# A semaphore wait in front of each of 432 embedding gathers

## What is computed

```python
e = jnp.stack([tbl_f[ids[:, f]] for f in range(40)], axis=1)      # (2048, 40, 32)
vi = e[:, _I_IDX, :]                                              # the 780 pairs i < j
vj = e[:, _J_IDX, :]
z = jnp.einsum('bke,kef,bkf->bk', vi, W, vj)                      # (2048, 780)
h = jnp.concatenate([z, dense_ctx], axis=1)
h = jnp.maximum(h @ W_top1 + b_top1, 0.0)                         # 512 wide
h = jnp.maximum(h @ W_top2 + b_top2, 0.0)                         # 256 wide
y = h @ W_top3
```

## Time and profile before

| | |
|---|---|
| timed runs, median of 3 | 634.8 us (633.32 to 635.27) |
| profiled execution, span from the first to the last instruction | 1130.1 us |
| profiled execution, own time around the span | not given; the span alone is known |
| mean granted clock of PE in the profile | 0.81 of full speed |
| busy in the profile: PE, VectorE, ScalarE, POOL | 875.4, 540.3, 327.1, 412.3 us |

### The profile page before, as it was taken

One profiled execution on the slowest core, in us unless ns is written; L12 is line 12 of the kernel. 1 busy time (PEld: TensorE's weight loads), 2 busy tenths in 40 slices (PEclk: granted clock), 3 DMA queues, 4 the chain that ended last, 5 costly groups with the idle time before them and its releaser, 6 DMA issues.

```text
span 1130.1 us, 16792 instructions
## 1 busy us (share of the span) xinstructions
PE 875.4 (77%) x7232; PEld 201.8 (18%) x7232; DVE 540.3 (48%) x510; ACT 327.1 (29%) x243; POOL 412.3 (36%) x436
## 2 busy tenths in 40 slices
PE   4322358788779995886895789779889787899998
PEld 1000012121112220121121112112112111122223
DVE  3100067364345660452380447337245264688884
ACT  4001047553246380032260134127244000000002
POOL 6777341533353137324517151451624604000000
PEclk8555598887578895886796788989779788899999
DMA  4100044201001020100101002010010102011010
GB/s 155 32 14 13 12 145 127 63 7 52 9 11 53 12 72 13 44 16 18 38 22 41 5 10 75 9 47 4 12 34 8 39 3 58 8 39 29 1 36 3
DMA packets 30489, 39.24 MB, mean 35 GB/s; under 512 B 11376, under 2 KB 19200, under 8 KB 30160
## 3 DMA queue, kind: packets, MB, share of 16 engines
q1 hardware_dynamic: 14880, 25.59, 7.7%
q0 software_dynamic: 13824, 7.11, 4.3%
q10 hardware_dynamic: 1712, 5.48, 1.4%
HBM read 21.93 MB, written 0.07 MB: 19 GB/s over the span
## 4 chain that ended last, share of the span: by engine, by line
PE 65%; another core or an unknown queue 17%; issue 11%; DVE 3%; ACT 2%; SPq 1%; DMA 1%; DVEq 0%; ACTq 0%
PE t_ps L857 27%; PE z_ps L881 18%; PE x_ps L898 10%; PE x_ps L806 7%; PE x_ps L911 2%; SPq L543 1%; DVE prod L727 1%; ACT one_hot L602 1%; PE t_ps L911 1%; DVE one_hot L689 1%; PE t_ps L898 1%; PE t_ps L829 0%; DVE z_sb L673 0%; ACT one_hot L605 0%
## 5 line engine op out<-in xcount | busy, mean ns | idle before, releaser
L727 DVE TENSOR_TENSOR prod<-t_ps,e_t 128x1024 f32<-128x1024 f32 x392 | 459.4, 1213 | 425.2 <-remote 300.6
L558 POOL DMA_INDIRECT rows<-cold_tables,idx x432 | 412.1, 954 | 550.1 <-DVE e_t L734 420.2
L857 PE MATMUL t_ps<-e_t,w_sb 32*64 32x512 f32 x3120 | 362.0, 658 | 73.8 <-issue 53.6
L881 PE MATMUL z_ps<-prod,select 128*32 128x512 f32 x1560 | 243.5, 639 | 21.7 <-issue 21.0
L602 ACT ACTIVATE one_hot<-hot_sb,row_number 128x2048 bf16<-128x2048 f16 (+1 forms) x75 | 140.6, 1875 | 110.3 <-remote 87.4
L898 PE MATMUL x_ps<-z_sb,w_sb 128*32 128x512 f32 x704 | 131.1, 635 | 24.4 <-issue 22.5
L605 ACT ACTIVATE one_hot<-one_hot 128x2048 bf16<-128x2048 bf16 (+1 forms) x75 | 134.3, 1791 | 2.4
L857 PEld LDWEIGHTS t_ps<-e_t,w_sb 32*64 32x64 f32 x3120 | 74.6, 136 | 323.0 <-issue 221.6
L806 PE MATMUL x_ps<-one_hot,tables 128*32 128x512 bf16 x1194 | 97.8, 402 | 27.3 <-issue 22.6
L806 PE MATMUL t_ps<-one_hot,tables 128*32 128x512 bf16 x198 | 45.3, 501 | 92.1 <-issue 87.9
L689 DVE TENSOR_SCALAR one_hot<-hot_sb,row_number 128x2048 bf16<-128x2048 f16 (+1 forms) x47 | 33.9, 744 | 133.2 <-remote 130.0
(11 more groups left out here) (33 smaller groups left out, 98.6 us busy)
## 6 DMA issues: line engine op xcount, KB each, us to landing
e_t<-e_t SPq DMA_DIRECT2D x64, 128.0 KB
e_t<-e_t SPq DMA_DIRECT2D x112, 64.0 KB
rows<-cold_tables,idx POOLq DMA_INDIRECT x432
hot_sb<-hot_ids SPq DMA_DIRECT2D x11, 512.0 KB, 3.6
w_sb<-w_lay ACTq DMA_DIRECT2D x1, 1792.0 KB, 7.0
z_sb<-hot_tables SPq DMA_DIRECT2D x4, 320.0 KB, 5.1
w_sb<-w_lay ACTq DMA_DIRECT2D x1, 1216.0 KB
w_sb<-w_lay ACTq DMA_DIRECT2D x1, 896.0 KB, 4.6
```

What stands on the lines that cost most here:

```text
L558: pool.indirect_dma_start(out=rows[:, slot, span, :], out_offset=None, in_=table, in_offset=bass.IndirectOffsetOnAxis(ap=idx[:, n, span:sp ...
L727: nc.vector.tensor_tensor(prod[:, u % PROD_SLOTS, 0:banks, :], t_ps[:, at:at + banks, :], by, ALU.mult).then_inc(mult_done, 1)
L857: mm = nc.tensor.matmul(t_ps[cols, at + n, :], w_sb[part, b, cols], e_t[part, e_slot(k, of[side]), :], start=True, stop=True)
L881: mm = nc.tensor.matmul(z_ps[E * q:E * q + E, :], select[:, E - PER - PER * s:2 * E - PER - PER * s], prod[:, (u + q // 2) % PROD_SLOTS, q ...
```

## The change

Each gather gets a place among the 837 steps. `PACE` gives the steps between which an item's 16 gathers lie: 0 to 54 for item 0, 54 to 100 for item 1, 100 to 130, 130 to 160, 160 to 190, 190 to 215 for the rest of chunk 0, and 25 steps for each later item, the last from 715 to 740; inside an item they are spaced evenly. Before a gather POOL looks back from its place for the last gen or lookup block and waits for that: for a gen until VectorE has multiplied both of its halves, for a lookup block until PE has finished it.

```diff
+PACE = [0, 54, 100, 130, 160, 190] + [215 + 25 * n for n in range(22)]
+
+
+def pace_of(n, span):
+
+    begin, end = PACE[n], PACE[n + 1]
+    return begin + (end - begin) * span // SPANS
...
+        def wait_for_pace(engine, place):
+
+            for kind, *of in reversed(steps[:place]):
+                if kind == "gen":
+                    engine.wait_ge(mult_done, first_unit(*of) + 2)
+                    return
+                if kind == "hot" and of[2] < blocks[of[1]] - 1:
+                    engine.wait_ge(looked_up, looked_up_to[tuple(of)])
+                    return
...
                 if n >= ROW_SLOTS:
                     pool.wait_ge(turned, n - ROW_SLOTS + 1)
                 for span in range(SPANS):
+                    wait_for_pace(pool, pace_of(n, span))
                     pool.indirect_dma_start(
```

## The result

The change takes 639.73 us (638.73 to 640.91, 4 runs) against 634.32 us: 1.0097 times the time before, 95% interval 1.0078 to 1.0116, so 5.4 us more. Repeated on another chip it was 639.32 against 635.46 (1.0062; 1.0041 to 1.0083), 3.9 us more.

A forecast was written before the change was run, and what follows sets the result against it. PE was taken to bound the timed execution, at work for 588 of 634.8 us, POOL close behind at 541. Waits 0, spacing 0 and start 0 to 2.1 us gave 635.5 us, range 625 to 646.

The forecast's parts named there:

- the lost lead: Slower rival, chance 0.33: POOL starts item 2 late, VectorE stands at turns of items 8, 10, 12; 8 us, 643 us.
- start 0 to 2.1 us: Term of the sum: POOL's later start makes later items late by 0 to 2.1 us.
- I take 0: Cost on POOL of a wait already met: 0 per gather, with 0.30 us kept for the range.
- Mostly nominal: Items 6 to 26: POOL needs 1.25 us per gather against places of 1.21, so it issues back to back as before.
- For item 0 ... two gathers and a landing, 5.1 us: not late: Item 0's turn, step 68: 8 us of VectorE's work after step 46 covers its last gather's 5.1 us.
- late by 2.1 us at most: Item 12's turn, step 416: its gathers come at most 2.1 us late, or in time.
- The head start: POOL's early lead at item 1's last gather: nothing, or up to 22 us of it, is lost by waiting for step 96.
- PE's sum of 588 us: PE's work over all 837 steps, from unit prices: 588 of the timed 634.8 us.
- faster rival: Chance 0.27: bursts also starve PE in timed executions, so spreading helps; floor 619 us, half the gain 627 us.
- G: All waiting PE has anyway from step 97 to 416: at least 7.4 us, subtracted from item 12's lateness of 9.5 us.
- A timed execution can't contain this in full: PE's stall beside gather bursts in the 1130.1 us profile can't fit fully into timed runs of 634.8 us.
- The rule on the shared port: VectorE's comparisons delay POOL's gathers: 3 us more from step 97 to 416, counted only in the slower rival.

The follow-up runs named there:

- f2: The kernel before plus one wait alone, that of item 0's 4th gather for the first finished lookup block: 639.21 us against 633.35, ratio 1.0097.
- f1: The changed kernel with item 0's 16 gathers waiting for nothing, items 1 to 26 keeping their waits: 633.1 us against 633.35 before, ratio 0.9995.
- g2: The changed kernel with the 1792 KB load of pair matrices issued with a later copy: 637.25 us against 633.39 before, ratio 1.0051.
- g1: The changed kernel with item 0's turn moved from step 68 to step 100: 636.98 us against 633.39 before, ratio 1.0050.
- i1: The changed kernel with item 0's turn at step 100 and the 1792 KB load issued later: 637.32 us against 634.45 before, ratio 1.0060.
- e4: The changed kernel with item 0's turn at step 100, under the slow condition: 875.6 us against 1132.3 before, ratio 0.7739.
- e1: The changed kernel with item 0's gathers waiting for nothing, under the slow condition: 877.7 us against 1132.3 before, ratio 0.7740.

## Why the prediction was right and wrong

The time was forecast at 635.5, within 625 to 646; it is 639.7, so the range held. That was luck: its upper part was there for the lost lead, and the loss came by a path that the prediction had ruled out. By its own words ("wrong if the time leaves 633 to 638 us; it would mean that the lead was needed") the forecast failed, and the meaning given was wrong too. The single most likely direction, no change (0.40), didn't come; slower (0.33) did. The sum's term "start 0 to 2.1 us" measured 5.4 and 3.9 us in the change and 5.9 us in f2. By its steps:

- **"I take 0" for a wait that is met**: right. f1 with 416 waits is 0.9995.
- **"Mostly nominal" spreading in the timed execution**: right under the fast condition. From item 1's last gather, 53.10, to item 12's, 276.17, are 176 gathers in 223.1 us, 1.267 us each; f2, which has no waits there, has 1.265.
- **"For item 0 ... two gathers and a landing, 5.1 us: not late"**: this step failed, and it is the result. I looked at the wait of the last gather and not at the sum of the stream before it. In f1 the last gather of item 0 starts at 24.39 and VectorE is at the turn at 33.25, so there was slack. In the change 3 gathers, a stand of 6.02 us and 12 pitches of 1.38 us ((31.07 - 14.48) / 12), not 1.254, bring it to 31.07, 6.7 us later, and use the slack up. The other half is the landing, which I put at 2.6 us and which was 6.8: the row I took it from was a load at the start, while this one stood behind 1792 KB. With a landing of 1.7 us, as in g2, VectorE would have waited some 0.4 us by the change's own times (an estimate: 32.08 + 1.7 against 33.33; g2 itself, with POOL 1 us later, had 1.84).
- **"If VectorE waits at the transpose for a DMA, that is the lost lead"**: such a wait came, but at item 0, and f1 and f2 tie it to the stand before the 4th gather.
- **Item 12 "late by 2.1 us at most"**: the place was right, the size about so. It shows only once item 0 is cured: 1.49 (g1), 1.40 (g2), and 1.00 and 2.68 us at items 10 and 12 (i1). In the change no wait is seen there.
- **The head start**: item 1's last gather starts at 53.10 against 46.89 in f1, so 6.2 us were lost, within the 0 to 22 given. They come from the same stand (f2, which has that one wait alone, has 52.21), not from the wait for step 96 to which I had put them.
- **PE's sum of 588 us and the faster rival's floor of 619 us**: too low. PE is busy for 614 us in the change. In f1, from 47 us, about item 1's last gather, to item 12's turn at 277 us it is busy for 226.3 of 230.0 us, where I had summed 215.1:

```profile
47.00:277.00 230.00, 226.27 (x2786) 58.73 (x2778) 205.64 (x191) 179.49 (x114) 173.99 (x182) 0.99 0.27 64
277.00:633.00 356.00, 352.54 (x4028) 87.20 (x4020) 294.57 (x268) 113.29 (x96) 207.78 (x219) 1.00 0.18 40
```

The lookup matmuls are most of the difference: 48.5 us for 696 there, 0.070 us each, not 0.054. Behind 47 us PE idles for 7 us in all, so the 16 us that this rival wanted to win weren't there. And 230 us are 14.9 more than the sum, where G of 9.5 was enough for item 12 to be in time: it is, in f1 and in the change, but G, PE's waiting, is only a small part of that.

- **"A timed execution can't contain this in full"**: wrong. Whole jobs run at 1132 and 1142 us. I took the gap between profile and times for an effect of profiling; the executions of those jobs are as long as the profile. The forecast of the profiled span, 700 to 950 us, missed the 638.4 of the fast condition for the same reason; under the slow one e4 had 861.4.
- **The rule on the shared port** (the Trainium skill, "SBUF — State Buffer", "Who interferes with whom": an instruction of VectorE in a two-port mode that was issued first blocks GpSimd for its whole length): the trace agrees in direction. The gather of 14.48 took 1.58 us against 0.95. Which instruction of VectorE held it isn't shown by a run. The slower rival says that it takes half of the 3 us of this, but its 8 us hold all 3.

## What to carry to other kernels

When a stream that is nearly saturated gets waits, look for the first place where it stands, not for the price of a wait: one stand of 6 us at the start made the whole loss, partly by pushing a gather behind a big load, and 416 waits that were met cost nothing measurable. Here it was enough to give the first consumer's item free rein and pace the rest: that cost nothing under the fast condition (f1) and took 23% off under the slow one (e1). And when a profile's span and the timed runs differ by a factor, time the kernel again in another job, on another chip too, before calling it an effect of the profiler.

## What the hardware showed unexpectedly

The same kernel takes some 634 us or over 1130 us, in whole jobs, and on one and the same chip 633.4 and 1142.3 us, with the same instructions and the same 1.25 us from gather to gather. Under the slow condition PE gets 23 matmuls through in 65 us beside 52 gathers. And a gather of 128 rows landed 1.4 to 1.7 us after POOL was done with it (g1, g2), 2.8 us at item 10 of i1, and 6.8 us in the change, where a load of 1792 KB had been issued 0.8 us before it.
